# Where the two halves of a tile's softmax sums are joined: masks on VectorE instead of GpSimd

## The reference

```python
scores = jnp.einsum('bqhd,bkhd->bhqk', q, k) / jnp.sqrt(jnp.float32(dh))
attn = jax.nn.softmax(scores, axis=-1)
out = jnp.einsum('bhqk,bkhd->bqhd', attn, v).reshape(B, Lq, H)
return x_q + (out @ Wp + bp)
```

## Time and profile before

| what | us |
|---|---|
| median of 3 runs | 437.07 (436.45 to 438.8) |
| the profiled execution, its own time | 438.55 |
| its span, from first to last instruction | 436.8 |
| TensorE busy in the span | 417.7 |
| VectorE busy | 283.2 |
| ScalarE busy | 220.0 |
| GpSimd busy | 190.3 |

### The profile page before, as it was taken

How to read it: one execution, slowest core, us unless ns; L and a number is a source line. 1 busy time by engine, 2 the same in 40 slices (tenths; PEclk the granted TensorE clock), 3 DMA queues, 4 the chain that set the end, 5 groups by cost and what they waited for, 6 DMA issues and landing times.

```text
span 436.8 us, 9535 instructions
## 1 busy us (share of the span) xinstructions
PE 417.7 (96%) x3581; PEld 379.9 (87%) x3581; DVE 283.2 (65%) x726; ACT 220.0 (50%) x487; POOL 190.3 (44%) x196
## 2 busy tenths in 40 slices
PE   7989999999999999999999999989999899979995
PEld 7578999989998899989998799879988898868874
DVE  2685566673766585748773877377557765781777
ACT  3778634245347633863367236723672366316271
POOL 6445473253543475326533663366335732441030
PEclk9899999999999999999999999999999999998999
DMA  9787001541200221124000400030003021300301
GB/s 296 239 290 281 26 2 42 159 91 30 45 4 2 57 65 29 26 56 138 2 5 13 109 2 5 13 86 2 5 19 81 0 49 32 81 5 26 72 2 50
DMA packets 16981, 27.67 MB, mean 63 GB/s; under 512 B 3816, under 2 KB 9256, under 8 KB 16808
## 3 DMA queue, kind: packets, MB, share of 16 engines
q1 hardware_dynamic: 16808, 27.06, 21.4%
q10 hardware_dynamic: 128, 0.01, 0.0%
HBM read 15.80 MB, written 2.10 MB: 41 GB/s over the span
## 4 chain that ended last, share of the span: by engine, by line
PE 81%; DVE 6%; POOL 5%; ACT 3%; issue 2%; SPq 0%; DMA 0%; POOLq 0%; ACTq 0%
PE hidden_banks L1729 8%; PE hidden_banks L1731 8%; PE hidden_banks L1730 8%; PE score_banks L1736 6%; PE token_bank L1729 6%; PE token_bank L1730 5%; PE token_bank L1731 5%; PE score_banks L2101 5%; PE value_bank L2124 3%; PE score_banks L2071 3%; PE value_bank L2127 3%; PE hidden_banks L1954 3%; PE value_bank L1736 3%; PE head_bank L1736 2%; PE score_banks L1810 1%
## 5 line engine op out<-in xcount | busy, mean ns | idle before, releaser
L1658 POOL TENSOR_TENSOR hidden_low<-hidden,hidden_high 128x512 fp32r<-128x512 f32 x56 | 72.6, 1297 | 133.0 <-ACT hidden_high L1084 133.0
L1485 DVE TENSOR_REDUCE head_maxima<-score_banks 128x2 f32<-128x308 f32 x128 | 54.0, 471 | 17.1 <-PE score_banks L2071 15.1
L1729 PE MATMUL hidden_banks<-normed_high,hidden_w_high 128*128 128x256 f32 x224 | 64.2, 287 | 0.9 <-issue 0.9
L1730 PE MATMUL hidden_banks<-normed_high,hidden_w_low 128*128 128x256 f32 x224 | 62.5, 279 | 0.0
L1731 PE MATMUL hidden_banks<-normed_low,hidden_w_high 128*128 128x256 f32 x224 | 62.4, 279 | 0.0
L1146 ACT ACTIVATE exp_ring<-score_banks 128x512 f32<-128x512 f32 x96 | 52.6, 600 | 19.2 <-PE score_banks L2101 18.3
L1076 ACT ACTIVATE hidden<-hidden_banks 128x512 f32<-128x512 f32 x56 | 33.3, 595 | 49.3 <-PE hidden_banks L1954 47.7
L1084 ACT CAST hidden_high<-hidden 128x512 fp32r<-128x512 f32 x56 | 34.8, 621 | 45.0 <-DVE hidden L1402 42.4
L1729 PE MATMUL token_bank<-expert_out_high,hidden_high 128*128 128x256 f32 x192 | 55.9, 291 | 1.5 <-POOL hidden_low L1658 1.4
L1730 PE MATMUL token_bank<-expert_out_high,hidden_low 128*128 128x256 f32 x192 | 53.5, 279 | 0.0
L1731 PE MATMUL token_bank<-expert_out_low,hidden_high 128*128 128x256 f32 x192 | 53.5, 279 | 0.0
(11 more groups left out here) (301 smaller groups left out, 1092.2 us busy)
## 6 DMA issues: line engine op xcount, KB each, us to landing
unit_weights<-units SPq DMA_DIRECT2D x7, 768.0 KB, 5.8
query_stack<-queries_high SPq DMA_DIRECT2D x56, 64.0 KB, 2.0
tokens<-x SPq DMA_DIRECT2D x8, 256.0 KB, 3.5
query_stack<-queries_low SPq DMA_DIRECT2D x28, 64.0 KB, 2.0
w_slice<-units SPq DMA_DIRECT2D x7, 256.0 KB, 2.9
out<-tokens SPq DMA_DIRECT2D x7, 256.0 KB, 2.4
w_T<-folds SPq DMA_DIRECT2D x6, 256.0 KB, 5.9
pair_keys<-keys_high SPq DMA_DIRECT2D x16, 77.0 KB
```

What stands on the lines that cost most here:

```text
L1485: v.tensor_reduce(MX[:, s, first:first + step + 1:step], S[:, ring_of[key][0], 0:2 * CTX].rearrange("p (j n) -> p j n", j=2), AX.X, ALU.ma ...
L1658: nc.gpsimd.tensor_tensor(SL[:, ring(t, u), :], TB[:, ring(t, u), :], raw(SH[:, ring(t, u), :]), ALU.subtract).then_inc(gpsimd_h, 1)
L1729: mm(out_, lh, rh, start=start, stop=False, skip_group_check=skip)
L1730: mm(out_, ll, rh, start=False, stop=False, skip_group_check=skip)
```

## The change

The additions of the four groups stay on GpSimd, one instruction per tile (tiles 0 to 6). The two masks and the second addition go to VectorE, in the form that the last tile has already: a `tensor_scalar` with one mask and a `scalar_tensor_tensor` that multiplies with the other mask and adds. The semaphore `gpsimd_part` and GpSimd's two waits on it are gone.

```diff
@@ VectorE @@
                 if t == LAST:
                     dve.wait_ge(scalar_raw, upto(scalar_raw, ("raw", t, h), "v"))
-                    v.tensor_scalar(total[:, :], RAWL[:, 2 * h, :], other_rows, None, ALU.mult).then_inc(vector_results, results.one())
-                    dve.wait_ge(vector_results, results.n)
-                    v.scalar_tensor_tensor(out=total[:, :], in0=RAWL[:, 2 * h + 1, :], scalar=own_rows, in1=total[:, :],
-                                           op0=ALU.mult, op1=ALU.add).then_inc(vector_results, results.one())
-                    dve.wait_ge(vector_results, results.n)
+                    even, odd = RAWL[:, 2 * h, :], RAWL[:, 2 * h + 1, :]
                 else:
                     dve.wait_ge(gpsimd_sum, upto(gpsimd_sum, ("sum", t), "s"))
+                    even, odd = (out_tiles(t)[0][:, o, :] for o in range(2))
+                v.tensor_scalar(total[:, :], even, other_rows, None, ALU.mult).then_inc(vector_results, results.one())
+                dve.wait_ge(vector_results, results.n)
+                v.scalar_tensor_tensor(out=total[:, :], in0=odd, scalar=own_rows, in1=total[:, :],
+                                       op0=ALU.mult, op1=ALU.add).then_inc(vector_results, results.one())
+                dve.wait_ge(vector_results, results.n)
                 v.reciprocal(total[:, :], total[:, :]).then_inc(vector_sums, 1)
@@ GpSimd @@
                 both = out_tiles(t)[0]
-                nc.gpsimd.tensor_tensor(both[:, :, :], RAW[:, 0:2, :], RAW[:, 2:4, :], ALU.add).then_inc(gpsimd_part, 1)
-                pool.wait_ge(gpsimd_part, 3 * t + 1)
-                nc.gpsimd.tensor_scalar(both[:, 0, :], both[:, 0, :], other_rows, None, ALU.mult).then_inc(gpsimd_part, 1)
-                nc.gpsimd.tensor_scalar(both[:, 1, :], both[:, 1, :], own_rows, None, ALU.mult).then_inc(gpsimd_part, 1)
-                pool.wait_ge(gpsimd_part, 3 * t + 3)
-                nc.gpsimd.tensor_tensor(SUM[:, :], both[:, 0, :], both[:, 1, :], ALU.add).then_inc(gpsimd_sum, 1)
+                nc.gpsimd.tensor_tensor(both[:, :, :], RAW[:, 0:2, :], RAW[:, 2:4, :], ALU.add).then_inc(gpsimd_sum, 1)
```

More of the change, by code:

```diff
@@ L673, in build @@
         vector_results = sem("vector_results")
-        gpsimd_part = sem("gpsimd_part")
         small_loaded = sem("small_loaded")
```

## The result

The changed kernel takes **433.71 us** in the median of five executions (433.55 to 434.58). The kernel before, executed beside it, took 438.24 us in the median of five (436.45 to 439.5; three of them are the ones that the prediction started from, with their median of 437.07). The ratio is 0.990, with a 95% interval of 0.988 to 0.993: by the ratio 4.2 us faster, and the two medians lie 4.5 us apart. What the prediction named as signs of its being right is there: no wait for `hidden_low` behind the addition, the pair at its forecast length, and tile 6 nearer to its copy by 0.96 us. How much each was worth, and why the ratio shows more than the forecast, is what the experiments were for.

The account below looks back on a forecast made before the run. TensorE, busy 417.7 of 436.8 us, bounds the kernel, and at the end VectorE's chain. Terms -1.4 (three waits), 0 (pair in six tiles), -0.9 (end) sum to -2.3: 437.07 to 434.8 us, range 433.8 to 438.0.

Parts of the forecast that it names:

- GpSimd, tiles 0, 2 and 3: TensorE's three waits of 0.46 us for `hidden_low`, behind GpSimd's join, go whole: -1.4 us.
- VectorE's 0.2 us: VectorE's reciprocal after the join starts 0.2 us earlier in tile 2 (246.91 instead of 247.14); not counted in the sum.
- Tiles 1, 4 and 5: Tiles where TensorE has no wait for `hidden_low` behind the join: nothing gained.
- VectorE, tiles 0 to 5: The added mask and masked addition, 0.90 us per tile, fit where VectorE waits 1.05 us for GpSimd: cost 0.
- the port rival: Tiles 0, 2, 3: GpSimd's `rstd` blocks L1503, then `hidden_low` blocks L1505; 1.8 us paid, 438.0 us total; chance 0.11.
- The end: Tile 6, VectorE's closing chain: the reciprocal starts earlier because VectorE no longer waits for GpSimd's join, -0.9 us.
- Only the end gains: Rival: TensorE's 0.46 us are taken back by the next wait in each of three tiles; 436.2 us; chance 0.22.
- Slower: Rival: the port rival plus L1520 blocked behind both `probs`; 1.4 us paid in tiles 0 to 3; 441.9 us; chance 0.07.

Follow-up runs that it names:

- the second trace before: The kernel before, unchanged, profiled and timed once more: median 437.02 us, ratio 0.9996; its profiled execution has a span of 434.3 us.
- the first six tiles alone: Against the kernel before, the join moved to VectorE in tiles 0 to 5 only, tile 6 stays on GpSimd: median 436.3 us, ratio 0.9966.
- the kernel with a busy GpSimd: The changed kernel plus two unused masks and an addition on GpSimd in tiles 0 to 5: median 437.48 us, ratio 0.9998 against the kernel before.

## Why the prediction was right, and where it was off

**GpSimd, tiles 0, 2 and 3: the mechanism right, the size too small.** The waits for `hidden_low` went whole, `hidden_low` started at 246.66 (forecast 246.82), and the next product stayed in time. But the term of -1.4 us took 0.46 us a wait from the bracket of the row. The starts give 0.63, 0.77 and 0.73, together -2.1 us. Two steps were off. Reading a row's idle time as the length of a wait, when the end of the work before it is a model, cost 0.15 us a wait (0.61 by the starts). And VectorE's 0.2 us, which the prediction had, were put at nothing: they bring the second product for the scores forward by 0.12 to 0.16 us in each of the three tiles, ahead of the expert product. Together this is 0.7 of the missing microsecond.

**Tiles 1, 4 and 5: forecast nothing, right for 1 and 4.** Tile 5 gave 0.3 us by the traces. The prediction had the cause in hand, VectorE earlier by 0.2 us, and gave it no value because it found no wait that it would shorten. It had allowed for it only in the lower end of the range.

**VectorE, tiles 0 to 5: right.** The pair took 0.34 and 0.48 us, and counted from the start of L1401 the reciprocal is 0.25 us earlier (1.74 before, 1.49 now), likewise in the other tiles except tile 1. There a `context_w_low` (L1190) stands between them, and the reciprocal comes 0.05 us later than before (1.77, now 1.82). The masks of the packed outputs did fall beside `probs`, as the port rival had it: L1520 took 815 ns in the mean of six before and L1521 takes 943, and `probs` grew from 616 and 450 to 714 and 726 ns. It cost 0.13 us a tile on VectorE (0.10 against the 847 ns of the second trace before), inside the cover.

**The end: right.** Forecast -0.9, measured -0.95, with L1521 at 0.75 us instead of 0.85, and with the room ahead of the second part used to 0.05 us.

**The rivals.** *Only the end gains* fell with the first six tiles alone: -2.3 us by the trace, ratio 0.9966 with an interval that excludes 1. *The port lost* had the order right up to its decisive link: `rstd` ran from 245.59, and L1503 was issued into it at 245.85. It took 0.34 us, its usual time. By the rule of the Trainium skill (SBUF — State Buffer, Who interferes with whom) `rstd` should have held it off until its end at 246.29; the trace disagrees for this small operation. *Slower* fell with it. Its other link, VectorE held up by large additions on GpSimd, is real, as the kernel with a busy GpSimd shows.

**The sum.** -2.3 forecast, about -3.3 measured at equal clock: 0.7 from tiles 0, 2 and 3, 0.3 from tile 5, 0.05 from the end. From 437.07 that is 433.8 us; that 433.71 was then measured so near to it owes something to luck, since four of those five executions had full clock. The base itself is loose by as much, since the kernel before has medians from 437.07 to 438.44 us by the mix of its executions' clocks.

## What to carry to other kernels

A wait of TensorE behind pipelined matmuls can be longer than the idle time its row shows; compare start to start, here 0.61 us for a bracket of 0.46, and look for waits with no bracket at all where a feeding engine moves. Before moving work between VectorE and GpSimd, ask what remains on the engine it leaves: the same added instructions were free with GpSimd relieved, and with it kept as busy as before nothing of the gain was left. Where a profiled execution is the base of a sum, take a second one of the same kernel and compare granted clocks, since one stretch at half clock weighs as much as half the change.

## What the runs showed of the hardware that was not expected

- One kernel has executions with a mean granted clock of 1.00 and of 0.988, with 436.74 and 439.28 us. The traces with less than full clock have stretches at 1.2 GHz, behind the wait of 2.19 us at 391 us (granted clock 0.83 from 390 to 400 us) or early in the kernel (0.83 from 10 to 20 us), and the first profile has both. The one at 391 us cost 1.4 us. Whether they come differs from execution to execution, and how often from kernel to kernel; what decides it stays open.
- Two DMA issues on SyncE's queue took 1.85 us in one execution and 2.48 in another, and TensorE's wait for what they bring appeared or not.
- A GpSimd operation of 128x2 (`rstd`, 0.70 us) did not hold VectorE's mask of 128x256 up, which was issued 0.26 us into it and took its usual 0.34 us. Nor did GpSimd's mask of 128x256 hold up VectorE's of 128x512, issued 0.37 us into it (its usual 0.47 us); that mask itself took 1.09 us for 0.92. The two other cases agree with a hold by whoever came first: GpSimd's next mask, issued 0.20 us into VectorE's masked addition, took 1.35 us and ended 0.80 us behind it, and GpSimd's additions with two inputs held VectorE until they ended (0.92 us for 0.48).
